# A quarter of two state-space scans' input products moved from VectorE to GpSimd, with two smaller moves to ScalarE and TensorE

## The chip, the cores and the metric

The program runs on one core of a Trainium2 chip. The metric is the device time of one execution in microseconds (us), median of several runs. A core has five engines with queues of their own that meet at semaphores: TensorE (PE in the profile, PEld its weight loads), VectorE (DVE), ScalarE (ACT), GpSimd (POOL) and SyncE (SP, which issues DMAs). SBUF is the working memory of 128 partitions; PSUM holds eight banks of 512 float32 columns, into which TensorE writes.

## The reference

The model is a decoder of four layers with three blocks each, twelve in all, on x of 16 sequences x 128 tokens x 256 features. The change touches two of the twelve, both state-space blocks: the first block of layer 1 (L1_attn, "mamba" in the code) and the first block of layer 3 (L3_attn, "sequence_ssm"). Of the first the reference computes

```python
xc = causal_depthwise_conv(x_inner, conv_w) + conv_b      # 4 taps, 512 channels
x_conv = silu(xc)
ssm = x_conv @ W_xproj;  dt_raw, Bp, Cp = ssm[..., :1], ssm[..., 1:17], ssm[..., 17:]
dt = softplus(dt_raw @ W_dt + b_dt);  A = -exp(A_log)
A_bar = exp(dt * A)                                        # one for each of 16 states
B_bar = (dt * x_conv)[..., None] * Bp[:, :, None, :]
h = A_bar_t * h + B_bar_t                                  # over the tokens
y = sum over states of h * C,  plus  x_conv * D
y = y * silu(z);  out = residual + y @ W_out
```

The second has the same recurrence with 256 channels, a 3-tap convolution across channels made by TensorE, and a normalization behind the gate.

## The kernel before

The twelve blocks run as twelve stages one after another, with a barrier between two. Within a state-space stage the 16 sequences go through in four groups of 4; the tokens of a group stand side by side, 512 columns. Channels lie on partitions, 128 to a block. L1_attn has 4 blocks of channels and takes them two at a time, so its scan runs over 4 groups x 2 halves x 16 states = 128 steps; L3_attn has 2 blocks and runs 4 x 16 = 64 steps. Sixteen steps with the same channels are called a unit here, and four steps in a row (0 to 3, 4 to 7, ...) a quartet.

`class Scan` holds what one step N does, on tiles of 128 x 1024 float32 (two blocks of channels by 512 columns):

- TensorE spreads the row of B for this state over all partitions into one PSUM bank ("brow", L1162) and the row of C into another ("crow"); each of the two has one bank only, and brow N+1 waits until brow N has been read.
- ScalarE makes the decay exp(dt*A) ("decay", two instructions, L1179, two buffers) and copies the row of C to SBUF ("ccol", L1185).
- VectorE multiplies dtx by the row of B into a pair of PSUM banks ("drive", L1195, one buffer) and runs the recurrence ("scan", L1203) with the decay from SBUF and the drive from PSUM; the state goes to one of three SBUF buffers.
- GpSimd multiplies the state by the row of C in place ("weigh", L1210).
- TensorE adds the weighed state to the unit's sum y in PSUM by two matmuls with the identity ("sum", L1168).

Behind the sixteenth sum VectorE runs "finish" (L1415, L1419 in L1_attn; L1711, L1715 in L3_attn): xc*D + y in two instructions, then times the gate. Around the scan stands the work of the next and the last group: the projections and their reads ("inner", "gate", "turn", "project", "delta", "out"; L1281, L1294, L1308), the convolution ("conv", in L1_attn one tensor_scalar L1392 and three scalar_tensor_tensor L1395 on VectorE for each block of channels), "silu" (two ACTIVATEs between two table loads, L1340 to L1342), "relu" (eight ACTIVATEs, L1353, L1354), "soften" (L1360, L1362), the norm's "stats" and "apply" (L241, L261), "rows" and "split" (L1400, L1143 to L1152), "step" and "strength" on GpSimd.

The order in which each engine issues all this is fixed by tables of due times (MAMBA_BY_STEP, MAMBA_BY_GROUP, SSM_BY_STEP and so on): all steps are sorted by due time, in units of a step, and every engine issues its own in that order. An engine never overtakes its own queue: when one instruction waits, all behind it wait.

## Time and profile before

| | us |
|---|---|
| median of 3 runs | 3912.26 |
| lowest and highest of them | 3909.07, 3914.52 |
| the profiled execution's own time | 3913.75 |
| its span | 3912.4 |
| stretch of L1_attn (1210 to 1845), VectorE busy in it | 635, of it 553.0 |
| stretch of L3_attn (3110 to 3500), VectorE busy in it | 390, of it 301.7 |

The span is the time from the first to the last instruction; the execution's own time is 1.35 us more. The page gives busy times of the whole program; since stages follow each other behind barriers, a stage's length counts in full, and what bounds it is read from its own stretch.

### The profile page before, as it was taken

Reading aid. Unit: us, or ns where it says so; the run is one execution under the profiler, and the core shown is the slowest. Engines: PE = TensorE matmul, PEld = TensorE weight load, DVE = VectorE, ACT = ScalarE, POOL = GpSimd, SP = SyncE. Lnnn points to the kernel's source line nnn. Section 1 sums busy time; section 2 is a strip of 40 time slices with the busy share of each in tenths; the row PEclk is TensorE's granted clock in tenths of the full one; section 3 lists DMA queues with packets and bytes.
Section 4 is the critical chain, followed back from the end, with each engine's and each line's share of the span. In section 5 each row is a group of like instructions: output and inputs, shape, how many; then the busy total and the mean of one; then the engine's idle time right before and its main releaser. Section 6 shows DMA issues by size and latency. Waiting matters only on the chain. (4 is left out here: it accounts for less than half of the span.)

```text
span 3912.4 us, 52926 instructions
## 1 busy us (share of the span) xinstructions
PE 3102.8 (79%) x17627; PEld 1971.6 (50%) x17627; DVE 2347.5 (60%) x6436; ACT 1637.3 (42%) x3689; POOL 1450.2 (37%) x1121
## 2 busy tenths in 40 slices
PE   6989986877942777775899999468789678868898
PEld 4666665656631232322666766245567423325655
DVE  6988984374333999997244343544542268874553
ACT  4776763211212556553344444315602145435521
POOL 3777774103443566564122222300010145640020
PEclk7999998888976999999999999789969888889999
DMA  3000000302442000000000000120121200000000
GB/s 100 6 10 7 10 10 22 127 22 78 128 117 86 0 1 0 1 0 16 2 8 1 1 1 1 20 85 26 39 92 29 60 23 1 1 30 2 2 1 22
DMA packets 70999, 116.10 MB, mean 30 GB/s; under 512 B 28688, under 2 KB 58408, under 8 KB 67984
## 3 DMA queue, kind: packets, MB, share of 16 engines
q1 hardware_dynamic: 61184, 86.63, 6.6%
q0 software_dynamic: 9552, 26.10, 2.7%
q8 instruction: 149, 2.44, 0.3%
q14 instruction: 114, 0.93, 0.1%
HBM read 88.71 MB, written 23.99 MB: 29 GB/s over the span
## 5 line engine op out<-in xcount | busy, mean ns | idle before, releaser
L1210 POOL TENSOR_TENSOR L_attn_state<-L_attn_state,L_attn_ccol 128x1024 f32<-128x1024 f32 x192 | 451.8, 2354 | 317.4 <-DVE L_attn_state L1203 242.6
L1168 PE MATMUL bank<-L_attn_state,ident 128*128 128x512 f32 x768 | 404.8, 652 | 90.5 <-POOL L_attn_state L1210 86.5
L1203 DVE TENSOR_TENSOR_SCAN L_attn_state<-L_attn_decay,bank 128x1024 f32<-128x1024 f32 x192 | 438.6, 2284 | 20.1 <-ACT L_attn_decay L1179 1.0
L1179 ACT ACTIVATE L_attn_decay<-L_attn_dt,L_attn_A 128x512 f32<-128x512 f32 x384 | 256.3, 717 | 128.4 <-DVE L_attn_state L1203 120.1
L1168 PEld LDWEIGHTS bank<-L_attn_state,ident 128*128 128x128 f32 x768 | 144.1, 201 | 272.2 <-POOL L_attn_state L1210 149.0
L1107 POOL TENSOR_TENSOR L_xattn_prob<-L_xattn_prob,L_xattn_inv 128x1024 f32<-128x1024 f32 x64 | 121.1, 1893 | 410.1 <-DVE L_xattn_inv L1090 410.1
L1195 DVE TENSOR_TENSOR bank<-L_attn_dtx,bank 128x1024 f32<-128x1024 f32 x192 | 235.6, 1227 | 44.9 <-PE bank L1162 20.3
L1185 ACT COPY L_attn_ccol<-bank 128x512 f32<-128x512 f32 x192 | 112.3, 585 | 226.0 <-PE bank L1162 179.2
L2758 POOL TENSOR_TENSOR L_attn_t<-L_attn_t,L_attn_base 128x1024 f32<-128x1024 f32 x96 | 182.5, 1901 | 37.5 <-DVE L_attn_base L2707 36.8
L1162 PE MATMUL bank<-L_attn_parts,L_attn_select 96*128 96x512 bf16 x384 | 128.2, 406 | 84.6 <-DVE bank L1195 80.8
L758 ACT ACTIVATE L_xattn_prob<-bank,L_xattn_top 128x128 f32<-128x128 f32 x512 | 142.0, 377 | 57.3 <-DVE L_xattn_top L807 56.9
L1032 ACT ACTIVATE L_xattn_prob<-L_xattn_masked,L_xattn_low 128x256 f32<-128x256 f32 x256 | 128.1, 507 | 83.5 <-DVE L_xattn_low L1085 83.5
L1085 DVE CUSTOM_DVE_ANT_0 L_xattn_masked<-bank,L_xattn_hidden 128x256 f32<-128x256 f32 x256 | 96.6, 419 | 105.1 <-PE bank L945 105.1
L2762 POOL TENSOR_TENSOR L_attn_t<-L_attn_t 128x512 f32<-128x512 f32 x96 | 122.0, 1271 | 97.8 <-ACT L_attn_t L2566 97.0
L2711 DVE MATCH_REPLACE8 L_attn_t<-L_attn_top,L_attn_t 128x64 f32<-128x64 f32 x768 | 150.2, 207 | 0.0
L1162 PEld LDWEIGHTS bank<-L_attn_parts,L_attn_select 96*128 96x128 bf16 x384 | 32.5, 102 | 227.0 <-DVE bank L1195 165.2
L3411 POOL DMA_INDIRECT L_ffn_xh<-L_ffn_rows,L_ffn_tokens x96 | 90.9, 947 | 142.0 <-PE bank L3216 80.1
L922 PE MATMUL bank<-L_xattn_kvT,L_xattn_wk 128*128 128x256 f32 x512 | 126.1, 389 | 10.8 <-ACT L_xattn_qT L1020 5.1
L931 PE MATMUL bank<-L_xattn_wv,L_xattn_kvT 128*128 128x512 f32 x256 | 126.9, 618 | 2.2 <-DVE L_xattn_kT L987 0.8
L807 DVE TENSOR_REDUCE L_xattn_top<-bank 128x4 f32<-128x512 f32 x128 | 82.5, 684 | 50.5 <-PE bank L666 50.5
L252 POOL TENSOR_TENSOR L_ffn_norm_rs<-L_ffn_norm_mv,eps 128x4 f32<-128x4 f32 x16 | 5.1, 318 | 289.4 <-DVE L_ffn_norm_mv L245 289.4
L922 PEld LDWEIGHTS bank<-L_xattn_kvT,L_xattn_wk 128*128 128x128 f32 x512 | 92.1, 190 | 32.0 <-ACT L_xattn_qT L1020 11.6
(597 smaller groups left out, 7463.0 us busy)
## 6 DMA issues: line engine op xcount, KB each, us to landing
L_ffn_ew<-in_L_ffn_experts SPq DMA_DIRECT2D x4, 3072.0 KB, 21.0
L_ffn_made<-L_ffn_yout SPq DMA_DIRECT2D x24, 512.0 KB, 2.9
L_ffn_w<-in_L_ffn_w SPq DMA_DIRECT2D x4, 2048.0 KB, 15.1
L_xattn_ctx<-in_ctx_rows SPq DMA_DIRECT2D x3, 2048.0 KB, 8.5
L_ffn_rows<-L_ffn_xh SPq DMA_DIRECT2D x8, 512.0 KB, 2.9
L_ffn_made<-L_ffn_yout SPq DMA_DIRECT2D x11, 256.0 KB, 2.1
L_attn_rows<-in_x SPq DMA_DIRECT2D x16, 128.0 KB, 7.2
turned<-L_attn_rows SPq DMA_DIRECT2D x16, 128.0 KB, 2.3
```

What stands on the lines that cost most here:

```text
L758: t = act.activation(prob[u % 2][j][:, i, :], score[j].bank(u)[:, i * P:(i + 1) * P], ACT.Exp, bias=top[:, j, i:i + 1])
L922: t = pe.matmul(side.bank(at)[:, i * 2 * P:(i + 1) * 2 * P], w["wk"][:, k, col:col + P], kvT[a % 2][:, k, :], start=k == 0, stop=k == KC - 1)
L931: t = pe.matmul(side.bank(at)[:, :], kvT[a % 2][:, k, half * P:(half + 1) * P], w["wv"][:, k, cols], start=k == 0, stop=k == KC - 1)
L1032: t = act.activation(prob[i % 3][:, h, :], masked[i % 2][:, h, :], ACT.Exp, bias=low[:, i % 2, h:h + 1], scale=-1.0, accum_out=total[:, i ...
L1162: pe.matmul(fills.bank(N)[:, :], self.select[:, first + n, :], parts[:, :], start=True, stop=True).then_inc(*fills.full.up())
L1168: t = pe.matmul(self.y[unit % len(self.y)][m][:, :], self.c.ident[:, :], self.state[N % 3][:, m, :], start=n == 0, stop=n == 15)
L1179: t = act.activation(self.decay[N % 2][:, m, :], dt[:, m, :], ACT.Exp, scale=A[:, m, n:n + 1])
L1195: dve.tensor_tensor(self.drive[:, :, :], dtx[:, :, :], self.brow.bank(N)[:, :].unsqueeze(1).broadcast_to([P, 2, GT]), ALU.mult).then_inc(* ...
L1203: dve.tensor_tensor_scan(flat(self.state[N % 3]), flat(self.decay[N % 2]), flat(self.drive), 0.0, ALU.mult, ALU.add).then_inc(*self.scanne ...
L1210: pool.tensor_tensor(state[:, :, :], state[:, :, :], self.ccol[N % 2][:, :].unsqueeze(1).broadcast_to([P, 2, GT]), ALU.mult).then_inc(*sel ...
L2711: m = dve.match_replace(t[n % RING][:, 1, i, :], top[n % 2][:, i, :], t[n % RING][:, 0, i, :], -1e30)
L2758: pool.tensor_tensor(both, both, base[n % 2][:, :].unsqueeze(1).unsqueeze(3).broadcast_to([P, 2, per, nkeys]), ALU.subtract).then_inc(*shi ...
```

## The change

Of each quartet of steps the fourth (N = 3, 7, 11, ...) gets its drive from another engine. ScalarE copies the row of B from its bank to SBUF ("bcol"), GpSimd multiplies dtx by the copy into one SBUF tile ("offer"), and VectorE's scan of that step reads both inputs from SBUF. The offer waits for the scan of the quartet before, which read the same tile, and for the copy. The state gets a fourth buffer, the decay a third.

In L1_attn the convolution's first tap with its bias becomes an ACTIVATE on ScalarE ("tap"), which writes xc; VectorE keeps the three others. In both stages the term xc*D becomes two matmuls with a diagonal matrix that open the unit's sum; the matrices are made by four (L1_attn) or two (L3_attn) tensor_scalar of 128 x 128 at the stage's start. "finish" is then one instruction, the sum from PSUM times the gate, and the next unit's sum waits for it. All tables of due times have new values.

```diff
 class Scan:
+    SHARE = 4
...
-        self.brow, self.crow = Fills(s, "brow", banks[0:1], "v"), Fills(s, "crow", banks[1:2], "a")
+        self.brow, self.crow = Fills(s, "brow", banks[0:1], "vvva"), Fills(s, "crow", banks[1:2], "a")
...
+    def shared(self, N):
+        return N % self.SHARE == self.SHARE - 1
...
+        for m in range(self.blocks):
+            dve.tensor_scalar(self.skip[:, m, :], self.c.ident[:, :], through(m), None, ALU.mult)
...
+            if n == 0:
+                for m in range(2):
+                    pe.matmul(self.y[unit % len(self.y)][m][:, :], self.skip[:, first_block + m, :], past[:, m, :], start=True, stop=False)
...
-            if N >= 2:
-                act.wait_ge(*self.scanned.at(N - 2))
+            if N >= 3:
+                act.wait_ge(*self.scanned.at(N - 3))
...
+        elif what == "bcol":
+            if N >= self.SHARE:
+                act.wait_ge(*self.offered.at(N // self.SHARE - 1))
+            act.wait_ge(*self.brow.filled(N))
+            act.copy(self.bcol[:, :], self.brow.bank(N)[:, :]).then_inc(*self.brow.done(N))
...
-        if what == "drive":
+        if what == "drive" and not self.shared(N):
...
-                dve.wait_ge(*self.scanned.at(N - 1))
+                dve.wait_ge(*self.scanned.at(N - 2 if self.shared(N - 1) else N - 1))
...
-            if N >= 3:
-                dve.wait_ge(*self.summed.at(N - 3))
+            if N >= 4:
+                dve.wait_ge(*self.summed.at(N - 4))
             dve.wait_ge(*self.decayed.at(N))
-            dve.wait_ge(*self.brow.emptied(N))
-            dve.tensor_tensor_scan(flat(self.state[N % 3]), flat(self.decay[N % 2]), flat(self.drive), 0.0, ALU.mult, ALU.add).then_inc(*self.scanned.up())
+            if self.shared(N):
+                dve.wait_ge(*self.offered.at(N // self.SHARE))
+                drive = self.offer
+            else:
+                dve.wait_ge(*self.brow.emptied(N))
+                drive = self.drive
+            dve.tensor_tensor_scan(flat(self.state[N % 4]), flat(self.decay[N % 3]), flat(drive), 0.0, ALU.mult, ALU.add).then_inc(*self.scanned.up())
...
+        if what == "offer":
+            if N % 16 == self.SHARE - 1:
+                pool.wait_ge(*ready)
+            if N >= self.SHARE:
+                pool.wait_ge(*self.scanned.at(N - self.SHARE))
+            pool.wait_ge(*self.brow.emptied(N))
+            pool.tensor_tensor(self.offer[:, :, :], dtx[:, :, :], self.bcol[:, :].unsqueeze(1).broadcast_to([P, 2, GT]), ALU.mult).then_inc(*self.offered.up())
+        elif what == "weigh":
...
-MAMBA_BY_STEP = {"brow": -1.68, "decay": -1.63, "crow": -0.36, "drive": -0.31, "ccol": -0.23, "scan": 0.17, "sum": 0.97, "weigh": 4.34}
+MAMBA_BY_STEP = {"brow": -1.77, "decay": -0.98, "crow": -0.8, "drive": -0.57, "scan": 0.32, "ccol": 0.73, "sum": 1.18, "weigh": 4.13}
+MAMBA_BY_SHARE = {"bcol": 2.15, "offer": 6.12}
...
+        elif what == "tap":
...
+            act.activation(xc[g % 2][:, m, :], side.bank(at)[:, :], ACT.Identity, bias=bias, scale=last).then_inc(*tapped.up())
...
         elif what == "finish":
             g, half = divmod(n, 2)
+            dve.wait_ge(*shaped.at(g))
             dve.wait_ge(*scan.summed.at(16 * n + 15))
-            for i in range(2):
-                m = 2 * half + i
-                t = dve.scalar_tensor_tensor(xc[g % 2][:, m, :], xc[g % 2][:, m, :], w["cols"][:, m, taps + 2:taps + 3], scan.y[0][i][:, :], ALU.mult, ALU.add)
-            t.then_inc(*finished.up())
-            dve.wait_ge(*shaped.at(g))
-            dve.wait_ge(*finished.at(n))
-            dve.tensor_tensor(halves(xc[g % 2], half), halves(xc[g % 2], half), halves(z[g % 2], half), ALU.mult).then_inc(*gated.up())
+            dve.tensor_tensor(halves(xc[g % 2], half), c.twins[0][:, :, :], halves(z[g % 2], half), ALU.mult).then_inc(*gated.up())
```

Three places show how the order moves. In all of them the scan is printed as SCALAR_TENSOR_TENSOR, the number behind L_attn_state tells the buffer (before 18127 to 18129, now 18128 to 18131, whose last is always a fourth step's), and bank stands for PSUM.

VectorE, steps 120 to 123 of L1_attn, before:

```order
L1195 TENSOR_TENSOR bank<-L_attn_dtx_18117,bank 128x1024
L1203 SCALAR_TENSOR_TENSOR L_attn_state_18127<-L_attn_decay_18125,bank 128x1024
L1195 TENSOR_TENSOR bank<-L_attn_dtx_18117,bank 128x1024
L1203 SCALAR_TENSOR_TENSOR L_attn_state_18128<-L_attn_decay_18126,bank 128x1024
L1195 TENSOR_TENSOR bank<-L_attn_dtx_18117,bank 128x1024
L1203 SCALAR_TENSOR_TENSOR L_attn_state_18129<-L_attn_decay_18125,bank 128x1024
```

and now:

```order
L1213 TENSOR_TENSOR bank<-L_attn_dtx_18117,bank 128x1024
L1226 SCALAR_TENSOR_TENSOR L_attn_state_18129<-L_attn_decay_18126,bank 128x1024
L1213 TENSOR_TENSOR bank<-L_attn_dtx_18117,bank 128x1024
L1226 SCALAR_TENSOR_TENSOR L_attn_state_18130<-L_attn_decay_18127,bank 128x1024
L1226 SCALAR_TENSOR_TENSOR L_attn_state_18131<-L_attn_decay_18125,L_attn_offer 128x1024
L1213 TENSOR_TENSOR bank<-L_attn_dtx_18117,bank 128x1024
```

The fourth step's drive is gone, its scan follows the third's directly, and the next quartet's drive stands behind it.

GpSimd at the same steps, before:

```order
L1210 TENSOR_TENSOR L_attn_state_18127<-L_attn_state_18127,L_attn_ccol_18130 128x1024
L1210 TENSOR_TENSOR L_attn_state_18128<-L_attn_state_18128,L_attn_ccol_18131 128x1024
L1210 TENSOR_TENSOR L_attn_state_18129<-L_attn_state_18129,L_attn_ccol_18130 128x1024
L1210 TENSOR_TENSOR L_attn_state_18127<-L_attn_state_18127,L_attn_ccol_18131 128x1024
```

and now:

```order
L1240 TENSOR_TENSOR L_attn_state_18128<-L_attn_state_18128,L_attn_ccol_18132 128x1024
L1240 TENSOR_TENSOR L_attn_state_18129<-L_attn_state_18129,L_attn_ccol_18133 128x1024
L1236 TENSOR_TENSOR L_attn_offer<-L_attn_dtx_18117,L_attn_bcol 128x1024
L1240 TENSOR_TENSOR L_attn_state_18130<-L_attn_state_18130,L_attn_ccol_18132 128x1024
L1240 TENSOR_TENSOR L_attn_state_18131<-L_attn_state_18131,L_attn_ccol_18133 128x1024
```

The offer stands between the second and the third step's weigh in every quartet of both stages.

TensorE at the end of L1_attn's third unit (steps 45 to 49); L_attn_w_ssm marks "project", which waits for silu, and L_attn_skip the new matmuls. Before:

```order
L1168 MATMUL bank<-L_attn_state_18129,ident 128x512 x2
L1162 MATMUL bank<-L_attn_parts_18119,L_attn_select_18124 128x512
L1294 MATMUL bank<-L_attn_xc_18112,L_attn_w_ssm 32x512 x2
L1162 MATMUL bank<-L_attn_parts_18119,L_attn_select_18124 128x512
L1168 MATMUL bank<-L_attn_state_18127,ident 128x512 x2
```

and now:

```order
L1326 MATMUL bank<-L_attn_xc_18112,L_attn_w_ssm 32x512 x2
L1181 MATMUL bank<-L_attn_state_18131,ident 128x512 x2
L1172 MATMUL bank<-L_attn_parts_18119,L_attn_select_18124 128x512 x2
L1178 MATMUL bank<-L_attn_xc_18113,L_attn_skip 128x512 x2
L1181 MATMUL bank<-L_attn_state_18128,ident 128x512 x2
```

Before, the project stood behind the unit's last sum (state 18129 is step 47's); now it stands ahead of it (18131 is step 47's).

## Rows read from the trace of the kernel before

**Rows 1.** The page's head: span, and busy time of each engine in the whole program.

```profile
span 3912.4 us, 52926 instructions
PE 3102.8 (79%) x17627; PEld 1971.6 (50%) x17627; DVE 2347.5 (60%) x6436; ACT 1637.3 (42%) x3689; POOL 1450.2 (37%) x1121
```

**Rows 2.** Busy time by stretch: L1_attn, then L3_attn; clock, DMA share, GB/s last.

```profile
1210.00:1845.00 635.00, 457.17 (x1120) 176.78 (x1120) 553.02 (x436) 325.59 (x490) 352.65 (x192) 0.93 0.02 8
3110.00:3500.00 390.00, 288.55 (x700) 118.10 (x700) 301.74 (x372) 175.11 (x286) 208.01 (x143) 0.86 0.04 10
```

**Rows 3.** Groups in L1_attn: busy us, mean ns | idle before, and its releasers.

```profile
L1210 POOL TENSOR_TENSOR L_attn_state<-L_attn_state,L_attn_ccol 128x1024 f32<-128x1024 f32 x128 | 301.3, 2355 | 210.0 <-DVE L_attn_state L1203 144.2 <-ACT L_attn_ccol L1185 65.6
L1203 DVE TENSOR_TENSOR_SCAN L_attn_state<-L_attn_decay,bank 128x1024 f32<-128x1024 f32 x128 | 292.5, 2285 | 15.4 <-ACT L_attn_decay L1179 1.0
...
L1195 DVE TENSOR_TENSOR bank<-L_attn_dtx,bank 128x1024 f32<-128x1024 f32 x128 | 157.1, 1227 | 16.6 <-POOL L_attn_dt L1467 10.7 <-PE bank L1162 1.7
...
L1392 DVE TENSOR_SCALAR L_attn_xc<-bank,L_attn_cols 128x512 f32<-128x512 f32 x16 | 12.8, 798 | 7.6 <-PE bank L1281 7.6
L1354 ACT ACTIVATE L_attn_soft<-bank,L_attn_cols,L_attn_w_dt 128x512 f32<-128x512 f32 x16 | 12.6, 789 | 0.0
...
L1415 DVE SCALAR_TENSOR_TENSOR L_attn_xc<-L_attn_xc,L_attn_cols,bank 128x512 f32<-128x512 f32 x16 | 11.2, 743 | 6.0 <-PE bank L1168 6.0
...
L1360 ACT ACTIVATE L_attn_soft<-L_attn_soft 128x1024 f32<-128x1024 f32 x8 | 8.5, 1057 | 0.0
...
L1400 DVE COPY L_attn_bc<-bank 32x512 f32<-32x512 f32 x4 | 2.7, 680 | 17.2 <-PE bank L1294 17.2
```

**Rows 4.** The same view of L3_attn: first the drives, then the finish's first part.

```profile
L1195 DVE TENSOR_TENSOR bank<-L_attn_dtx,bank 128x1024 f32<-128x1024 f32 x64 | 78.5, 1226 | 28.3 <-PE bank L1162 18.6 <-POOL L_attn_dt L1791 7.9
...
L1711 DVE SCALAR_TENSOR_TENSOR L_attn_h<-L_attn_h,L_attn_cols,bank 128x512 f32<-128x512 f32 x8 | 5.6, 744 | 5.4 <-PE bank L1168 5.4
```

**Rows 5.** Timeline of one plain step of L1_attn: start us, duration us, engine, instruction.

```profile
1809.15 1.23 DVE L1195 TENSOR_TENSOR bank<-L_attn_dtx,bank 128x1024 f32<-128x1024 f32 x1
1809.26 2.35 POOL L1210 TENSOR_TENSOR L_attn_state<-L_attn_state,L_attn_ccol 128x1024 f32<-128x1024 f32 x1 [1.33 <-DVE L_attn_state L1203]
...
1810.43 0.60 PE L1162 MATMUL bank<-L_attn_parts,L_attn_select 96*128 96x512 bf16 x2 [0.46 <-DVE bank L1195]
1810.51 2.29 DVE L1203 TENSOR_TENSOR_SCAN L_attn_state<-L_attn_decay,bank 128x1024 f32<-128x1024 f32 x1
1811.13 0.58 ACT L1185 COPY L_attn_ccol<-bank 128x512 f32<-128x512 f32 x1 [0.65 <-PE bank L1162]
...
1811.66 1.98 PE L1168 MATMUL bank<-L_attn_state,ident 128*128 128x512 f32 x4 [0.62 <-POOL L_attn_state L1210]
...
1812.83 1.23 DVE L1195 TENSOR_TENSOR bank<-L_attn_dtx,bank 128x1024 f32<-128x1024 f32 x1
```

**Rows 6.** All executions of L1985, with two SBUF inputs: ns min/median/max.

```profile
L1985 DVE SCALAR_TENSOR_TENSOR L_ffn_h<-L_ffn_h,L_ffn_h x32: 691/693/1886, 3726.7 to 3888.6; 128x512 f32<-128x512 f32 x32
```

**Rows 7.** Timeline of the last stage: VectorE's L1985 beside GpSimd's L2006, L2008, L2010.

```profile
3739.84 1.89 POOL L2006 TENSOR_TENSOR L_ffn_twice<-L_ffn_val,L_ffn_bo 128x1024 f32<-128x1024 f32 x1 [15.29 <-DVE L_ffn_hot L1954]
...
3740.40 1.88 DVE L1985 SCALAR_TENSOR_TENSOR L_ffn_h<-L_ffn_h,L_ffn_h 128x512 f32<-128x512 f32 x1
...
3741.81 2.22 POOL L2008 TENSOR_TENSOR L_ffn_twice<-L_ffn_twice 128x1024 f32<-128x1024 f32 x1
...
3742.91 1.67 DVE L1985 SCALAR_TENSOR_TENSOR L_ffn_h<-L_ffn_h,L_ffn_h 128x512 f32<-128x512 f32 x1
...
3744.11 2.69 POOL L2010 TENSOR_TENSOR X<-X,L_ffn_twice 128x1024 f32<-128x1024 f32 x1
```

**Rows 8.** Timeline of L1_ffn: VectorE starts 0.08 us behind GpSimd.

```profile
2495.38 2.12 POOL L2157 TENSOR_TENSOR L_ffn_yb<-L_ffn_yb,L_ffn_bias 128x1024 bf16<-128x1024 bf16 x1 [7.43 <-ACT L_ffn_yb L2111]
2495.46 2.59 DVE L2138 TENSOR_SCALAR L_ffn_over<-L_ffn_big 128x1024 f32<-128x1024 fp8e4 x1
```

**Rows 9.** Timeline of L1_attn: apply, beside two weighs in a row.

```profile
1290.80 4.69 POOL L1210 TENSOR_TENSOR L_attn_state<-L_attn_state,L_attn_ccol 128x1024 f32<-128x1024 f32 x2
...
1292.15 3.50 DVE L261 TENSOR_SCALAR L_attn_xn<-X,L_attn_norm_mv,L_attn_norm_rs 128x256 f32<-128x256 f32 x2
```

**Rows 10.** ScalarE's timeline at a silu.

```profile
1495.62 1.28 ACT L1340 ACT_TABLE_LOAD   x1
1496.91 1.91 ACT L1340 ACTIVATE L_attn_xc<-L_attn_xc 128x2048 f32<-128x2048 f32 x1
```

More of the change, by code:

```diff
@@ L1479, in ssm_weights @@
             ("a_log", name + "_a_log", [P, KC, NSTATE], F32), ("select", "select", [6 * NSTATE, 2 * NSTATE], F32)]
[L1482 to L1488 removed]
+SSM_BY_STEP = {"decay": -2.15, "weigh": -1.52, "drive": -1.23, "brow": -0.98, "crow": -0.55, "scan": -0.46, "ccol": -0.23, "sum": 1.78}
+SSM_BY_SHARE = {"offer": -0.22, "bcol": 1.77}
+SSM_BY_GROUP = {"stats": -25.24, "square": -19.99, "root": -18.09, "whole": -16.63, "wholes": -16.43, "apply": -15.55, "turned": (-14.21, -12.6),
+                "turn": (-13.85, -13.01), "inner": (-10.8, -9.91), "pad": (-10.61, -10.39), "shift": -10.46, "conv": (-9.86, -9.1),
+                "rooted": (-9.38, -9.13), "moved": -8.34, "normal": (-8.32, -8.1), "back0": -8.05, "convs": (-7.81, -7.41), "ranks": -7.11,
+                "rows": -6.81, "silu": -6.3, "rank": -6.1, "project": -5.77, "delta": (-5.72, -4.33), "step": -5.54, "strength": -5.44,
+                "split": -4.51, "relu": (-4.22, -3.91), "soften": -3.61, "finish": 16.03, "moments": (16.85, 17.44), "back": (17.83, 18.39),
+                "lastroot": 18.2, "last": 19.26, "out": (19.42, 20.18), "add": (19.74, 21.11)}
 def sequence_ssm(c, s, w, name, taps=3, rank=16):
@@ L1573, in tensor @@
             unit = n // 16
[L1574 removed]
+            scan.tensor(what, n, parts[unit % 2], scan.parted.at(unit), gated.at(unit - 1) if unit else None, h[unit % 2], 0)
         elif what == "back":
```

119 lines of the change are left out of this document (59 added, 60 removed).

## The prediction

> **What bounds the kernel now.** I read the page's head first [rows 1]: VectorE is the busiest engine but TensorE, at 60% of the span. Stages follow behind barriers, so what counts is each of the two stretches [rows 2]. In L1_attn VectorE is busy 553.0 of 635 us, in L3_attn 301.7 of 390, GpSimd 352.7 and 208.0: VectorE bounds both, GpSimd has room. The groups say with what [rows 3]: 128 scans of 2285 ns and 128 drives of 1227 ns. Then one plain step in order of time [rows 5]: a drive starts at 1809.15, the next at 1812.83, so a step lasts 3.68 us: drive 1.23, scan 2.29, two handovers of together 0.16. The weigh (2.35) waits for its scan [rows 3, 5] and is hidden. The execution took 3913.75, which is 1.35 over its span and 1.5 over the median; I sum against it and take 1.5 off at the end.
>
> **A plain quartet, step by step.** Let D be the end of the third step's drive. Before: third scan D+0.13 to 2.42, fourth drive 2.45 to 3.68, fourth scan 3.81 to 6.10.
>
> After, first the offer's own chain. The fourth brow is free to start at D+0.05 and takes a matmul, about 0.35 (two take 0.60, rows 5). The copy to SBUF takes as long as ccol's, 0.58, and ends near D+1.12. GpSimd is not free then: the second step's weigh starts 0.11 behind its scan's end, which is D−1.25 or so, and ends at D+1.22. So the offer runs 1.25 to 3.60. No row shows a GpSimd product with a broadcast SBUF operand except the weigh, which has this very form and size, so I price the offer at 2.35. The scan could start at D+3.65 and end at 5.94, **0.16 earlier** than now. The drive taken away (1.23) is thus nearly all given back as a wait for GpSimd.
>
> Second, the fourth scan reads decay and offer, both in SBUF; the plain scan has one input in PSUM. The trace has no such scan, but it has another VectorE operation with two SBUF inputs, L1985: 691 ns at least, 1886 at most [rows 6]. In the long cases GpSimd was at work [rows 7]: L2006 ends at 3741.73, and L1985, started at 3740.40, ends at 3742.28, 0.55 later, about its own 0.69. The second ends at 3744.58, again 0.55 behind L2008's end (3744.03). It waited for the whole GpSimd instruction. The other way holds too: L2010, started during such an L1985, took 2.69 where its like take 1.9 to 2.2. And where GpSimd starts first by only 0.08, VectorE's instruction is the one that is held [rows 8].
>
> The place: at the offer's end the third weigh stands directly behind it in GpSimd's queue, and all it waits for has been there since D+2.5. Two weighs in a row are recorded as 4.69 for both [rows 9], with no gap; a VectorE instruction released by GpSimd starts about 0.05 later. So the weigh is first, 3.60 to 5.95, the scan is held and ends 2.29−0.14 behind it, at 8.10 instead of 6.10: **+2.0 us for a plain quartet**.
>
> The Trainium skill, "SBUF — State Buffer", § Who interferes with whom, says the same for a DVE instruction with two SBUF inputs against a GpSimd instruction that reads SBUF, and that whoever issues first has the pair for its whole instruction. Its page "Advanced Engine Details and Errata", § VectorE Performance Modes, names only "2p Vector instructions" as blocked; by that, an fp32 scan would run free and the sum would be that of the second case below; rows 6 and 7 speak against it.
>
> **The quartets of L1_attn, 32.** Where other VectorE work stands in the quartet, GpSimd gets its weighs and the offer done meanwhile.
> - 21 have none: 21 × 2.0 = +42.
> - 8 have conv, stats, or rows and split: the offer is ready beforehand, the scan follows the third one and starts before the weigh, so each gains the drive with its handover, 1.33: −10.6. If they collide as well, 8 × 2.0 more.
> - 3 have apply, which by itself blocks and is blocked by GpSimd (3.50 for two, the weighs 4.69 beside it, rows 9): +0.8 each, +2.5.
>
> **The other parts in L1_attn.**
> - Tap: 16 tensor_scalar of 798 ns leave VectorE [rows 3]. The first four, in the prologue, wait for TensorE anyway (7.6 idle before the sixteen): 0. The other 12 × 0.80 = −9.6. ScalarE is busy 326 of 635 [rows 2] and takes 12 × 0.8, the price of relu's ACTIVATE of that shape from a bank (789).
> - Finish: two instructions of 743 go and one handover, two-input 128x1024 from PSUM stays like a drive: 8 × 1.35 = −10.8. For it TensorE makes 16 more matmuls of 512 columns, 0.5 each by the sum's 1.98 for four [rows 5]. TensorE is busy 457 of 635; they open the sum when the bank is free, hidden.
> - Rows waits 17.2 for its project now [rows 3], part of it outside the prologue; the new table puts it five steps later: −3.4. Set-up matrices: +1.
> - New stalls. Project now stands ahead of the unit's last sum on TensorE, and project waits for silu: decay, table load 1.28, 1.91 [rows 10], project 1.9, then sum 1.98, and finish behind it: 3 × 1.15 = +3.5. Relu's eight ACTIVATEs and soften's 1057 stand ahead of the next decay: with one decay of lead gained by the third buffer I get 3 × 2.5 = +7.5. Out ahead of sum and brow: +3. Brow late behind the new inner order: +2.5. Together +16.5; from 0 (the third buffer covers all) to 25.
>
> L1_attn: 42 − 10.6 + 2.5 − 9.6 − 10.8 − 3.4 + 1 + 16.5 = **+27.6**.
>
> **L3_attn, 16 quartets.** Its drives already wait 28.3 in all, 18.6 of it for brow [rows 4]. Three are plain (+6). Four have some VectorE work, half covered (+2). Three have rows or ranks beside them (−3). In three, at the turn of a unit, strength and the norm's powers stand on GpSimd ahead of the offer, and brow stands behind whole; the scan waits for two GpSimd instructions more: +6, +6, +4. Three with moments: +1. Finish, 4 × (2 × 0.744 plus a handover, less what waits for the last sum, 5.4 in all [rows 4]) is −2. Together **+20**.
>
> **Sum.** 27.6 + 20 = +47.6; 3913.75 + 47.6 − 1.5 = 3959.9, so **3960**, 1.2% slower. Own range: if the stalls don't come (−16.5) and L3's unit turns cost nothing (−16) 3928; if the eight covered quartets and three of L3 collide too (11 × 2.35 = +26), and a few us of stalls come on top, 3990.
>
> **Rivals.**
> - *The shared scan isn't held*: it goes in first, or two SBUF inputs don't block a scan. Then plain quartets gain 0.16 (21 × 0.16 = −3.4), apply costs nothing, L1_attn is −3.4 − 10.6 − 22.8 + 16.5 = −20.3. L3_attn: 20 less 6.5 (plain), 3 (half covered), 6 (turns) and 1: +3.5. Together −16.8: **3896**. This ends on the other side; it decides on 0.09 us, the handover to VectorE against GpSimd's own next instruction. For it: in rows 7 a VectorE instruction that was waiting got in before L2008. Against: L2008 was itself waiting for L2006's result; the weigh waits for nothing. 0.12.
> - *As that, and the third decay buffer covers the new stalls*: −33, **3879**. 0.03. VectorE would then really be lighter by what it lost.
> - *The blocking reaches the covered quartets as well*: GpSimd runs 160 weighs and offers at 2.35 in some 650 us, more than half the time, so a shared scan that comes at any moment is likelier than not to find one running. Against: in those eight the scan's place is right behind the third scan, ahead of the weigh that this one releases. +26: **3986**, within my range. 0.15.
> - *The clock*: TensorE is granted 0.93 and 0.86 in the two stretches [rows 2]. Longer waits in every quartet could bring it down; sums and brows, now hidden under a 3.68 us step, would then be 4 us each. In plain quartets its idle time grows from some 1.1 to 1.6 us a step. I take it as a small part of the stalls above, with no case of its own.
>
> **How the numbers follow.** Held scans 0.85 (0.70 as summed, 0.15 with the covered ones), the other two 0.12 and 0.03. The likeliest gives 3960. The range must reach the 0.12 case: **3890 to 3990**; below it lies the 0.03, above it a tail of the stalls, beside a share of the first rival's spread. A measurement can tell some 0.2%, 8 us. Faster: 0.03 + 0.10; same: 0.02 of the second case and 0.03 where the held scans cost half of what I say; slower: 0.82.
>
> **What would show it.** The 48 shared scans as a group by their form: mean near 4.4 us where they collide, 2.3 where not, and idle before them of 1.2 behind the offer. The timeline of a plain quartet: offer, weigh at once, scan's end 2.15 behind the weigh's. Offers of 2.35. Idle before finish (behind sum), before the scans of the steps behind relu (behind decay), and the wait for offer at L3's unit turns. The tap near 0.8 and the finish near 1.25 with no wait. It is wrong if the shared scans have a mean below 3 us, or if they start ahead of the third weigh.

## The result, and the profile after

| | before | after |
|---|---|---|
| median, us (4 runs each) | 3913.16 | 3959.56 |
| lowest and highest | 3909.07, 3914.52 | 3958.05, 3963.91 |
| ratio, 95% interval | | 1.0124, 1.0108 to 1.014 |
| profiled span | 3912.4 | 3956.8 |
| first to last scan of L1_attn | 552.3 | 579.8 |
| first to last scan of L3_attn | 311.5 | 337.3 |

The change makes the kernel slower by 46 us, 1.2%; the forecast was 3960. The two stretches from the start of the first scan to the end of the last give +27.5 and +25.8 us, together 53.3; outside them the profiled run is some 9 us shorter than before (3.2 ahead of the first scan, 3.0 between the stretches, 2.9 behind them). The stretches are the measure below: what lies between them holds of the change only L1_attn's last finish and L3_attn's set-up, and still takes anything from 1340.7 to 1349.7 us in the kernels below, so a median alone would hide small terms.

The page's head after, to be held against [rows 1]:

```profile
span 3956.8 us, 53092 instructions
PE 3134.2 (79%) x17675; PEld 1985.4 (50%) x17675; DVE 2330.3 (59%) x6354; ACT 1664.0 (42%) x3753; POOL 1597.6 (40%) x1169
```

VectorE is busy 17 us less and the program is 44 us longer. GpSimd has 147 us more; only 113 of them are the 48 offers (2.355 each), of the rest 24 are longer weighs (in L1_attn 313.8 instead of 301.3, in L3_attn 161.7 instead of 150.5) and 8 longer products for dtx. What VectorE does in L1_attn between its first and last scan is the view that answers to [rows 3] (groups, here with VectorE alone: busy us, mean ns | idle before, its releasers):

```profile
L1226 DVE TENSOR_TENSOR_SCAN L_attn_state<-L_attn_decay,bank 128x1024 f32<-128x1024 f32 x96 | 219.2, 2283 | 11.8 <-ACT L_attn_decay L1192 2.8 <-DVE bank L1213 0.5
L1226 DVE TENSOR_TENSOR_SCAN L_attn_state<-L_attn_decay,L_attn_offer 128x1024 f32<-128x1024 f32 x32 | 118.6, 3706 | 35.8 <-POOL L_attn_offer L1236 35.7
L1213 DVE TENSOR_TENSOR bank<-L_attn_dtx,bank 128x1024 f32<-128x1024 f32 x95 | 116.0, 1221 | 17.6 <-PE bank L1172 15.7
L261 DVE TENSOR_SCALAR L_attn_xn<-X,L_attn_norm_mv,L_attn_norm_rs 128x256 f32<-128x256 f32 x12 | 9.8, 872 | 0.0
...
L1452 DVE TENSOR_TENSOR L_attn_xc<-bank,L_attn_z 128x1024 f32<-128x1024 f32 x7 | 8.6, 1222 | 2.6 <-PE bank L1181 2.6
...
L1438 DVE COPY L_attn_bc<-bank 32x512 f32<-32x512 f32 x3 | 2.0, 653 | 0.0
```

The same view of before has for the drives and for the finish's first part:

```profile
L1195 DVE TENSOR_TENSOR bank<-L_attn_dtx,bank 128x1024 f32<-128x1024 f32 x127 | 155.9, 1227 | 5.9 <-PE bank L1162 1.7
...
L1415 DVE SCALAR_TENSOR_TENSOR L_attn_xc<-L_attn_xc,L_attn_cols,bank 128x512 f32<-128x512 f32 x14 | 9.8, 742 | 1.4 <-PE bank L1168 1.4
```

Read together, L1_attn's 27.5 us are: drives 155.9 to 116.0, −39.9; waits for the offer +35.7, with other waits before scans down by 3.6 (15.4 to 11.8); scans 292.5 to 337.8, **+45.3**, though their number is the same 128; waits before drives 5.9 to 17.6, +11.7; taps −9.5; finish −9.8 busy (the first parts are gone), +0.5 waiting; rows' wait −4.1; apply +2.6. (These add up to 29; records of instructions in a row overlap by some hundredths each.) The scans that got longer are the 32 that read the offer, mean 3706 against 2283 ns of the others.

One quartet, L1_attn's last, in order of time (start us, duration us, engine, instruction):

```profile
1842.63 1.23 DVE L1213 TENSOR_TENSOR bank<-L_attn_dtx,bank 128x1024 f32<-128x1024 f32 x1
1842.74 2.34 POOL L1240 TENSOR_TENSOR L_attn_state<-L_attn_state,L_attn_ccol 128x1024 f32<-128x1024 f32 x1 [1.33 <-DVE L_attn_state L1226]
...
1843.99 2.29 DVE L1226 TENSOR_TENSOR_SCAN L_attn_state<-L_attn_decay,bank 128x1024 f32<-128x1024 f32 x1
1844.39 0.59 ACT L1198 COPY L_attn_bcol<-bank 128x512 f32<-128x512 f32 x1 [2.37 <-PE bank L1172]
...
1845.12 2.34 POOL L1236 TENSOR_TENSOR L_attn_offer<-L_attn_dtx,L_attn_bcol 128x1024 f32<-128x1024 f32 x1
...
1847.42 2.34 POOL L1240 TENSOR_TENSOR L_attn_state<-L_attn_state,L_attn_ccol 128x1024 f32<-128x1024 f32 x1
...
1847.60 4.31 DVE L1226 TENSOR_TENSOR_SCAN L_attn_state<-L_attn_decay,L_attn_offer 128x1024 f32<-128x1024 f32 x1 [1.32 <-POOL L_attn_offer L1236]
```

D is 1843.86. The offer starts at D+1.26 and the scan at D+3.74. The third weigh started 0.18 before the scan and ends at 1849.76; the scan ends at 1851.91, 2.15 later, D+8.05. A plain quartet, one in which VectorE has nothing but drives and scans, lasts 16.56 instead of 14.72 to 14.79.

In ten quartets of L1_attn the scan comes first. In seven of them VectorE had other work ahead, so that the offer was ready. In the other three (1, 9 and 17, counted from 0 as everywhere below) VectorE waited for the offer, but the third weigh still waited for its copy of the row of C and started 0.60 behind the offer's end, when the scan, 0.13 behind it, had begun. The quartet with the four convs of L1_attn's first unit:

```profile
1318.90 2.35 POOL L1236 TENSOR_TENSOR L_attn_offer<-L_attn_dtx,L_attn_bcol 128x1024 f32<-128x1024 f32 x1
...
1319.75 2.28 DVE L1226 TENSOR_TENSOR_SCAN L_attn_state<-L_attn_decay,bank 128x1024 f32<-128x1024 f32 x1
...
1321.94 2.27 DVE L1226 TENSOR_TENSOR_SCAN L_attn_state<-L_attn_decay,L_attn_offer 128x1024 f32<-128x1024 f32 x1
1322.17 6.51 POOL L1240 TENSOR_TENSOR L_attn_state<-L_attn_state,L_attn_ccol 128x1024 f32<-128x1024 f32 x2 [0.92 <-DVE L_attn_state L1226]
```

Here the scan has its 2.27 and the two weighs take 6.51 instead of 4.69 [rows 9]: now they are held. Of the 32 shared scans of L1_attn 22 lasted 4.31 to 4.47 and 10 lasted 2.26 to 2.29; of L3_attn's 16 it was 8 and 8 (the short ones 2.25 to 2.29).

### The profile page after: what moved, and what is told of

Read it like the earlier page. It is cut to its first block and busy times, and to the rows that moved or that the text cites. A ratio compares the mean times of both kernels' runs of the same rounds, so it can differ in the third digit from the quotient of the medians.

```text
span 3956.8 us, 53092 instructions
## 1 busy us (share of the span) xinstructions
PE 3134.2 (79%) x17675; PEld 1985.4 (50%) x17675; DVE 2330.3 (59%) x6354; ACT 1664.0 (42%) x3753; POOL 1597.6 (40%) x1169
## 5 line engine op out<-in xcount | busy, mean ns | idle before, releaser
L1240 POOL TENSOR_TENSOR L_attn_state<-L_attn_state,L_attn_ccol 128x1024 f32<-128x1024 f32 x192 | 475.4, 2480 | 199.7 <-DVE L_attn_state L1226 164.4
L1181 PE MATMUL bank<-L_attn_state,ident 128*128 128x512 f32 x768 | 430.7, 689 | 127.4 <-POOL L_attn_state L1240 127.2
L1226 DVE TENSOR_TENSOR_SCAN L_attn_state<-L_attn_decay,bank 128x1024 f32<-128x1024 f32 x144 | 328.7, 2282 | 15.2 <-ACT L_attn_decay L1192 2.8
L1181 PEld LDWEIGHTS bank<-L_attn_state,ident 128*128 128x128 f32 x768 | 154.5, 213 | 321.1 <-POOL L_attn_state L1240 185.7
L1213 DVE TENSOR_TENSOR bank<-L_attn_dtx,bank 128x1024 f32<-128x1024 f32 x144 | 175.8, 1221 | 47.0 <-PE bank L1172 26.8
L1226 DVE TENSOR_TENSOR_SCAN L_attn_state<-L_attn_decay,L_attn_offer 128x1024 f32<-128x1024 f32 x48 | 171.3, 3569 | 53.8 <-POOL L_attn_offer L1236 46.3
L1172 PE MATMUL bank<-L_attn_parts,L_attn_select 96*128 96x512 bf16 x384 | 136.5, 409 | 78.4 <-DVE bank L1213 45.3
L922 PE MATMUL bank<-L_xattn_kvT,L_xattn_wk 128*128 128x256 f32 x512 | 126.1, 389 | 10.8 <-ACT L_xattn_qT L1020 5.1
L1236 POOL TENSOR_TENSOR L_attn_offer<-L_attn_dtx,L_attn_bcol 128x1024 f32<-128x1024 f32 x48 | 113.0, 2354 | 21.0 <-ACT L_attn_bcol L1198 20.0
```

What stands on the lines that cost most here:

```text
L922: t = pe.matmul(side.bank(at)[:, i * 2 * P:(i + 1) * 2 * P], w["wk"][:, k, col:col + P], kvT[a % 2][:, k, :], start=k == 0, stop=k == KC - 1)
L1172: pe.matmul(fills.bank(N)[:, :], self.select[:, first + n, :], parts[:, :], start=True, stop=True).then_inc(*fills.full.up())
L1181: t = pe.matmul(self.y[unit % len(self.y)][m][:, :], self.c.ident[:, :], self.state[N % 4][:, m, :], start=False, stop=n == 15)
L1213: dve.tensor_tensor(self.drive[:, :, :], dtx[:, :, :], self.brow.bank(N)[:, :].unsqueeze(1).broadcast_to([P, 2, GT]), ALU.mult).then_inc(* ...
L1226: dve.tensor_tensor_scan(flat(self.state[N % 4]), flat(self.decay[N % 3]), flat(drive), 0.0, ALU.mult, ALU.add).then_inc(*self.scanned.up())
L1240: pool.tensor_tensor(state[:, :, :], state[:, :, :], self.ccol[N % 2][:, :].unsqueeze(1).broadcast_to([P, 2, GT]), ALU.mult).then_inc(*sel ...
```

## The experiments

Eleven kernels, each timed against the kernel before on the same chip. Stretches are those of the first to the last scan, in us, each from one profile. L3_attn's code is the same in e4 and e9 and took 305.4 and 309.1, so differences under 4 us there show nothing; L1_attn's is the same in e3 and e9 and took 540.2 and 540.0.

| | ratio, 95% interval | L1_attn | L3_attn |
|---|---|---|---|
| before | | 552.3 | 311.5 |
| after | 1.0124 (1.0108 to 1.014) | 579.8 | 337.3 |
| e1, shared scan reads a bank | 0.9926 (0.9909 to 0.9942) | 543.3 | 309.4 |
| e2, third weigh behind the scan | 1.0184 (1.0167 to 1.0201) | 598.0 | 346.7 |
| e3, no sharing | 0.9918 (0.9902 to 0.9935) | 540.2 | 309.0 |
| e4, no sharing, old due times | 0.9945 (0.9929 to 0.9962) | 549.7 | 305.4 |
| e5, e2 with later sums | 1.0216 (1.0197 to 1.0236) | 591.5 | 360.6 |
| e6, shared row early | 1.0282 (1.0261 to 1.0303) | 580.3 | 398.9 |
| e7, before with tap | 0.9973 (0.9963 to 0.9983) | 544.6 | 312.8 |
| e8, before with skip | 0.9988 (0.9978 to 0.9997) | 558.0 | 305.4 |
| e9, no sharing, a table each | 0.9940 (0.9925 to 0.9955) | 540.0 | 309.1 |
| e10, small fill ahead of the weigh | 1.0157 (1.0138 to 1.0177) | 590.1 | 339.9 |
| e11, e10 with rows ahead of sums | 1.0245 (1.0228 to 1.0262) | 598.6 | 366.7 |

**e1: is it the two SBUF inputs?**

```diff
             if self.shared(N):
                 dve.wait_ge(*self.offered.at(N // self.SHARE))
-                drive = self.offer
+                drive = self.drive
```

(The next drive waits for this scan too.)

> The changed kernel, but each fourth scan takes its drive from the PSUM pair that the third step's drive has filled, and not from GpSimd's tile in SBUF; it still waits for the offer, which is made as before, and only its result isn't used (so those steps' states are not the reference's). Theory (the scan is held because both of its inputs are in SBUF): all 48 shared scans last 2.29; 29 of them lasted 4.3 to 4.5, so 29 x 2.05 = 59 us go, 3900 +- 6. Rival (the scan is long for another reason, such as the wait for the offer or GpSimd being busy at all): the shared scans stay near 4.3 in plain quartets and the time near 3960.

The ratio times 3913 is 3884, 76 us under the changed kernel against 59 expected (30 scans had been held, not 29). The scans in L1_attn's stretch, all of one form now:

```profile
L1226 DVE TENSOR_TENSOR_SCAN L_attn_state<-L_attn_decay,bank 128x1024 f32<-128x1024 f32 x128 | 292.1, 2284 | 45.3 <-POOL L_attn_offer L1236 33.4 <-ACT L_attn_decay L1192 2.8 <-DVE bank L1213 0.5
```

The mean is 2284 for all 128, though GpSimd makes every offer and weigh and the wait for the offer is still there (33.4). The weighs of L1_attn are back at 300.7 us as well. Only the place of one input and the next drive's wait changed, so the 4.3 us are due to the two SBUF inputs. The stretches fall by 36.5 and 27.9, together 64. In L1_attn the scans give 45.7 and longer waits before drives and finish take part of it back; in L3_attn the scans give 16.9, and another 6.2 come from a second instruction with two SBUF inputs, split's TENSOR_TENSOR (L1155): 2.72 each in the changed kernel, 0.68 here and before. e1 also says what the sharing is worth with the hold gone: 852.7 for both stretches, against 849.1 without sharing (e3). The drive that VectorE gives away comes back as the wait.

**e2: does the order at the offer's end decide?**

```diff
             pool.wait_ge(*self.crow.emptied(N))
-            pool.wait_ge(*self.scanned.at(N))
+            pool.wait_ge(*self.scanned.at(N + 1 if self.shared(N + 1) else N))
```

> The changed kernel, with one wait more: the weigh of each third step waits for the fourth step's scan, so that GpSimd starts nothing between the offer's end and that scan. Theory (who starts first holds the other, and the scan loses by the handover): the scan runs 2.29 right behind the offer, plain quartets last 14.56 instead of 16.56, 29 x 2.0 = 58 us less; two weighs and two sums come later, which may cost a few us at finish and at the unit turns: 3903, 3895 to 3925. Rival (the shared scan is slow beside GpSimd whatever the order, or the two late weighs hold up the next quartet's offer): 3940 to 3965.

The time is a miss: slower than the changed kernel, not 57 us faster, and above the rival's 3965 too. Of the mechanism the first half came: all 48 shared scans last 2.25 to 2.29, and quartets 11 and 19 of L1_attn take 14.61. Near the stretch's end the trace shows what took its place:

```profile
1848.72 2.29 DVE L1226 TENSOR_TENSOR_SCAN L_attn_state<-L_attn_decay,L_attn_offer 128x1024 f32<-128x1024 f32 x1 [1.34 <-POOL L_attn_offer L1236]
...
1851.16 4.65 POOL L1240 TENSOR_TENSOR L_attn_state<-L_attn_state,L_attn_ccol 128x1024 f32<-128x1024 f32 x2 [2.57 <-DVE L_attn_state L1226]
...
1853.56 3.78 PE L1181 MATMUL bank<-L_attn_state,ident 128*128 128x512 f32 x4 [4.89 <-POOL L_attn_state L1240]
1857.13 1.06 PE L1172 MATMUL bank<-L_attn_parts,L_attn_select 96*128 96x512 bf16 x2
...
1858.30 1.23 DVE L1213 TENSOR_TENSOR bank<-L_attn_dtx,bank 128x1024 f32<-128x1024 f32 x1 [3.74 <-PE bank L1172]
```

TensorE stands 4.89 us at the third step's sum, with the next rows of B and C queued behind it; then the sum takes 3.78 instead of 1.98, since the granted clock of that stretch is 0.50 (the lower of its two levels, 1.2 GHz) where the steps around have 1.00 (2.4 GHz). The next drive waits 3.74 for its row.

```profile
1853.50:1857.20 3.70, 3.64 (x5) 1.38 (x6) 1.06 (x1) 0.00 (x0) 2.31 (x2) 0.50 0.00 0
1860.96:1862.90 1.94, 1.94 (x6) 0.75 (x5) 1.91 (x2) 1.82 (x3) 0.81 (x1) 1.00 0.00 0
```

(Length; busy time of PE, PEld, DVE, ACT, POOL; granted clock; DMA share, GB/s.) Before it fell TensorE had been idle for 4.89 us, since the two rows that ended at 1848.67.

**e10: the same question with a tenth of a microsecond.**

```diff
             pool.tensor_tensor(self.offer[:, :, :], ...).then_inc(*self.offered.up())
+            pool.memset(self.spacer[:, :], 0.0)
```

> The changed kernel with one small instruction more: GpSimd fills a tile of 256 columns that nobody reads, between the offer and the third step's weigh. Nothing else waits for it, so it only moves the weigh's start by a few tenths of a us behind the offer's end, past the 0.13 at which the scan starts. Theory (whoever starts first has both inputs' way for its whole instruction): all 48 shared scans last 2.29, and it is the weigh that is held, its record 2.1 longer; the late weigh then holds the third step's sum and the rows queued behind it, as in the run with the explicit wait, so the time is about that run's, 3991, 3970 to 4000. Rival (a scan with two SBUF inputs is slowed by whatever GpSimd does, in either order): shared scans stay near 4.3, time near 3960 + 48 x 0.3 = 3974.

```profile
1846.13 0.32 POOL L1238 MEMSET L_attn_spacer<- 128x256 f32 x1
...
1846.33 2.29 DVE L1227 TENSOR_TENSOR_SCAN L_attn_state<-L_attn_decay,L_attn_offer 128x1024 f32<-128x1024 f32 x1 [1.33 <-POOL L_attn_offer L1237]
1846.40 6.66 POOL L1242 TENSOR_TENSOR L_attn_state<-L_attn_state,L_attn_ccol 128x1024 f32<-128x1024 f32 x2
```

The scan starts 0.07 before the weigh and has its 2.29; the two weighs take 6.66. In the changed kernel the weigh was 0.18 ahead and the scan took 4.31. So whichever starts first keeps the way for its whole length, and it is shown from both sides: here all 48 shared scans start ahead of the next weigh and last 2.25 to 2.29; in the changed kernel each of the 30 held ones starts 0.03 to 0.19 behind a weigh. The fill, which only writes, held nobody: the scan started in the middle of it and was not longer. The total, 3975 on the chip where before took 3913.5, is within what was expected, but the rival's total (3974) is too, so it is the scans' length that decides between them. VectorE's wait before drives in L1_attn is why nothing is won:

```profile
L1214 DVE TENSOR_TENSOR bank<-L_attn_dtx,bank 128x1024 f32<-128x1024 f32 x95 | 116.1, 1222 | 63.8 <-PE bank L1173 62.5
L1227 DVE TENSOR_TENSOR_SCAN L_attn_state<-L_attn_decay,L_attn_offer 128x1024 f32<-128x1024 f32 x32 | 73.1, 2286 | 34.4 <-POOL L_attn_offer L1237 34.3
```

46 us gained on the scans, 46 lost before the drives (17.6 to 63.8), 7 more at the finish.

**e5 and e11: can TensorE's order give it back?** e5 makes the sums due later in e2, e11 the rows of B earlier in e10.

```diff
-MAMBA_BY_STEP = {"brow": -1.77, ..., "sum": 1.18, "weigh": 4.13}
+MAMBA_BY_STEP = {"brow": -1.77, ..., "sum": 1.3, "weigh": 4.13}      # e5; second stage 1.78 to 2.05
+MAMBA_BY_STEP = {"brow": -1.85, ..., "sum": 1.18, "weigh": 4.13}     # e11; second stage -0.98 to -1.25
```

> The run with the weigh behind the shared scan was slower, though its shared scans lasted 2.29 and some quartets 14.61: in the others TensorE stood at the third step's sum, which waits for the late weigh, and the next row of B was queued behind it, so the next drive waited 3.7. Here the same kernel with the sums due 0.12 (second stage 0.27) of a step later, which puts the next rows ahead of that sum. Theory (the order of TensorE took back what the order of GpSimd gave): nearly all plain quartets 14.6, scans' stretches together some 865 instead of 945, 3908, 3895 to 3925. Rival (two weighs in a row behind the scan are themselves too late, by the buffers or GpSimd's load): over 3940.

> The run with the small fill between offer and weigh, and in TensorE's order one thing more: each row of B stands one place earlier, ahead of the sum of three steps before instead of behind it (due 0.08 earlier in the first stage, 0.27 in the second); sums and all else keep their places. Theory (what the free scan won was lost at the rows queued behind the late sum): VectorE's 63.8 us of idle before drives in the first stage fall to about 20, plain quartets are 14.5 throughout, the first stage's stretch is near 550 and the time 3925, 3905 to 3945. Even then it isn't under the run without sharing (3890), since the scan still waits some 1.3 for each offer. Rival (the late weigh is itself what binds): no less than 3960.

Both totals are misses, by 87 and 84 us. In e5 seven plain quartets of L1_attn are what was expected, 14.51 to 14.55, but the first quartet of six of the seven later units takes 22.6 to 24.9 and of the last 19.4 (17.8 to 19.7 in the changed kernel). In e11 the wait before drives did fall from 63.8 to 18.0, and came up elsewhere:

```profile
L1214 DVE TENSOR_TENSOR bank<-L_attn_dtx,bank 128x1024 f32<-128x1024 f32 x95 | 116.2, 1223 | 18.0 <-PE bank L1173 16.0
L1227 DVE TENSOR_TENSOR_SCAN L_attn_state<-L_attn_decay,L_attn_offer 128x1024 f32<-128x1024 f32 x32 | 73.2, 2288 | 56.0 <-POOL L_attn_offer L1237 49.9 <-PE bank L1182 6.0
...
L1454 DVE TENSOR_TENSOR L_attn_xc<-bank,L_attn_z 128x1024 f32<-128x1024 f32 x7 | 8.6, 1225 | 29.8 <-PE bank L1182 29.8
```

The finish waits 29.8 instead of 10.0. In TensorE's order a row now stands ahead of the unit's last two sums, and in four of the seven units it waits 3.65 for a drive, with the sums queued behind it; in the three others the project stands there too. The scans wait 56.0, 49.9 of it for offers. In these two attempts one due time for all steps did not serve both a plain quartet and a unit's end. My reading of e10 as "only the rows behind the late sum" was too narrow: with the rows out of the way the wait came back at the finish and before the offers, so the late weigh costs there as well.

**e6: sharing with the row first.** ScalarE's copy is made from the second row of a quartet, the offer stands between two pairs of weighs, the third step's weigh waits for the shared scan as in e2, and a table of four due times each for rows and sums follows.

```diff
+        return N - N % self.SHARE + (0, 2, 3, 1)[N % self.SHARE]        # place of a step's row in the bank
...
-MAMBA_BY_SHARE = {"bcol": 2.15, "offer": 6.12}
+MAMBA_BY_SHARE = {"bcol": -0.1, "offer": 3.6, "brow": (-2.1, -0.2, 0.1, 1.35), "crow": (-0.85, 0.7, 1.4, 2.5), "sum": (2.14, 2.8, 4.22, 4.8)}
```

> An attempt to make sharing pay: the shared step's row of B is the second of its quartet in the bank, not the fourth, so ScalarE's copy is early; GpSimd's order is weigh, weigh (third and fourth step of the quartet before), offer, weigh, weigh; the third step's weigh waits for the shared scan; rows and sums of TensorE are put where these come free. A plain quartet then costs GpSimd 5 x 2.35 and the scan's 2.15 to itself, 13.95, against 14.72 of before and 16.56 of the changed kernel. If it works 0.75 x some 45 quartets under the kernel without sharing (3890): 3857, 3840 to 3890. If the tight order makes new waits at the quartets with other work, 3890 to 3930; the plain quartets' length tells the mechanism by itself.

A few plain quartets came near the plan: 13.90 in L3_attn, and 13.91, 14.21 and 14.52 among those of L1_attn's last two units, at best 0.8 under before. The order isn't what it should be either: 15 of the 48 shared scans still last 2.5 to 3.9. The total is a miss by 166 us: the third quartets of L3_attn's first three units, those with rows and ranks, take 43.6 to 45.3, against 29 to 32 before. So sharing won up to 0.8 us in single plain quartets, and this order lost far more elsewhere; which part of it lost that was not taken apart.

**e3, e4, e9: the change without sharing.**

```diff
     def shared(self, N):
-        return N % self.SHARE == self.SHARE - 1
+        return False
```

(No bcol, no offer, every row emptied by VectorE. e4 has the due times of before in both stages, e9 in the second stage.)

> The changed kernel without the sharing: all drives on VectorE again, no bcol, no offer; tap on ScalarE, skip term on TensorE, three decay and four state buffers and all new due times stay. By the terms of the sum, tap -9.6 and some -3 in the prologue, finish -10.8 and -2, rows -3.4, set-up +1, stalls of the new order +16.5: 3913 - 11 = 3902. If the stalls don't exist without the sharing: 3886. Rival (tap and skip bring nothing on the path): 3913 to 3930.

> As the run without the sharing, but with the due times of the kernel before (tap just ahead of its conv). Tap -9.6 and -3 in the prologue, finish -10.8 and -2, set-up +1, no new stalls and no gain at rows: 3913 - 24 = 3889. The difference to the run with the new due times is what these cost by themselves: 13 by my terms. If the new due times cost nothing by themselves, both give the same.

> No sharing, tap on ScalarE and skip term on TensorE, the new due times in the first stage and those of before in the second. The scans' stretches were 540.2 (new due times) and 305.4 (old ones) in the two runs that had each: together 845.6 against 863.7 of before and 849.1 of the run with new due times in both. So 18 under before by the stretches, some 4 under the run without sharing; ratio 0.994 or below. If other stages' noise is larger, 0.991 to 0.998.

All three are faster than before, by 0.8, 0.55 and 0.6%; e3 and e9 can't be told apart and are the best kernels of this study. The sharing alone is thus the changed kernel less e3: 39.6 + 28.3 = 68 us in the stretches (the ratios, 1.0124 and 0.9918, say 81 of the total), and the rest of the change is worth −15 us in the stretches (the ratio of e3 says −32 of the total). e3 came out at 3890 where 3902 was expected, e4 at 3899 where it was 3889. The new due times gain 9.5 us in L1_attn without the sharing where I had them cost 13. For e9 the 3.6 us that e4's L3_attn had been shorter did not come back: the same code took 305.4 in one run and 309.1 in another, so that step of the expectation rested on noise; its total, 0.9940, is as expected.

**e7 and e8: tap alone, skip alone**, each with the due times of before.

> The kernel before with the first tap on ScalarE alone. By my terms 12 x 0.80 = 9.6 less in the scan's stretch and some 3 less ahead of it: 3913 - 12 = 3901. If conv waits for ScalarE instead (a tap queued behind a decay), under 4 us less.

> The kernel before with the skip term on TensorE alone (with the four state and three decay buffers of the changed kernel). By my terms 8 x 1.35 = 10.8 in the first stage and 2 in the second less, set-up +1: 3913 - 12 = 3901. In the run with both edits and the old due times every second quartet behind a finish was 1.7 longer than before, so part is given back there: 3 to 4 us of it.

The tap is worth 7.7 us in the stretch (expected 9.6), and the ratio gives 10.6 (3899 measured, 3901 expected). The skip term is worth 5 us by its ratio, 0.9988 (3905 measured, 3901 expected, 3 to 4 more if part is given back). L3_attn is 6.1 shorter, not much more than the same code varies, but L1_attn becomes 5.7 *longer*. Finish falls from 2.7 to 1.2 as expected, and in VectorE's groups this appears beside it:

```profile
L1213 DVE TENSOR_TENSOR bank<-L_attn_dtx,bank 128x1024 f32<-128x1024 f32 x127 | 155.8, 1227 | 12.8 <-PE bank L1172 8.9
...
L1448 DVE TENSOR_TENSOR L_attn_xc<-bank,L_attn_z 128x1024 f32<-128x1024 f32 x7 | 8.5, 1220 | 1.5 <-PE bank L1181 1.5
...
L1434 DVE COPY L_attn_bc<-bank 32x512 f32<-32x512 f32 x3 | 2.0, 679 | 13.8 <-PE bank L1326 13.8
```

Rows waits 13.8 for its project instead of 4.1, drives wait 12.8 instead of 5.9. The turn behind L1_attn's third unit shows how:

```profile
1500.91 1.88 PE L1178 MATMUL bank<-L_attn_xc,L_attn_skip 128*128 128x512 f32 x4
...
1502.63 1.88 PE L1181 MATMUL bank<-L_attn_state,ident 128*128 128x512 f32 x4
...
1504.44 1.90 PE L1326 MATMUL bank<-L_attn_xc,L_attn_w_ssm 128*32 128x512 f32 x4
...
1506.38 0.68 DVE L1434 COPY L_attn_bc<-bank 32x512 f32<-32x512 f32 x1 [4.49 <-PE bank L1326]
```

The skip matmuls stand ahead of sum and project on TensorE; before, the project started at 1502.82 and rows at 1504.76, with a wait of 1.26. VectorE reached this place earlier by the shorter finish, and waits until TensorE is through. With the new due times (e3) rows waits nothing, as rows stands five steps later.

## Why the prediction was right

The mechanism forecast as the likeliest is the one that occurred, and that the kernel becomes about 1% slower follows from it. That the number was right to a microsecond is luck, as its own steps show:

- **The sum.** e3 parts each stretch. In L1_attn the sharing is worth +39.6 (42 − 10.6 + 2.5 = 33.9 said) and the rest −12.1 (−6.3 said): two errors of 6 us that cancel. In L3_attn the sharing is worth +28.3 (22 said) and the rest −2.5 (−2 said). Together the stretches grew by 53.3 where 47.6 was said, and what lies outside them, for which next to nothing was said, came out some 9 shorter in the profiled run, which no run explains.
- **The quartet's clock held**: offer from D+1.26 (1.25), scan's start D+3.74 (3.65), end D+8.05 (8.10). The handover from GpSimd's product to the scan is 0.13, not 0.05 (behind GpSimd's small instructions the trace of before has 0.03 to 0.10), so the scan loses the race by more than I took. A plain quartet grew by 1.84 at most, not 2.0: the held scan ends 0.05 earlier than I said, and the next drive, which no longer waits for the scan just ahead of it, starts 0.08 before that scan's recorded end instead of 0.03 behind it.
- **The hold held.** e1 removes it by the place of one input, e2 and e10 by the order of the starts, with both inputs still in SBUF. L1985's 0.55 behind GpSimd's end [rows 7] was the right row to read: the held scan ends 2.15 behind it, 0.14 less than its own 2.29, as there.
- **The count held, its members did not.** 22 scans of L1_attn were held. Of the 21 quartets that I took as plain 18 were, the other three being those in which the weigh waited for its row of C; of the 8 that I took as covered the two with stats were held (4.41 and 4.32), and six kept their 2.27 to 2.29, with the weigh held instead; of the three with apply two were held.
- **The stalls of +16.5 were of about the right size (14.0) and of the wrong kind.** Waits for decays rose by 1.8 (7.5 said) and the finish waited 0.5 more (3.5 said); what came was +11.7 before the drives. That the skip matmuls are part of it is likely, not shown: with the old due times the skip term makes it 6.9 [e8], with the new ones and no sharing it is 6.8 [e3]. In e1, where no hold covers it, the finish does wait 9.1, 7.0 of it in the three units where the project stands ahead of the last sum: twice what I said for that. In the changed kernel, with its longer quartets, most of it was hidden.
- **Finish and rows.** Finish −9.8 busy for the seven within the stretch (−10.8 said for eight) and rows −4.1 (−3.4 said); but in e8, with rows at its old place, finish's gain is lost again at rows. That moving rows alone brings it back is argued; e3 moves all due times at once. I had called the skip matmuls hidden; with the old order they were not. I had also counted 16 of 0.5 each, but a matmul of the code is two records in the trace (rows 5 has four for the sum's two): the trace has 32, together 17.5 us, twice what I took. That step was wrong in its reason.
- **Prologue**: 3.2 us less in the profiled run (I said 0 and +1). But the kernels with the tap on ScalarE have their first scan anywhere from 1266.1 to 1276.6, and the two without it at 1272.5 and 1275.3, so it is not shown.
- **L3_attn +25.8, said +20, by errors that cancel.** The four quartets that I took as half covered (1, 5, 9, 13; said +2) were held, all four, and are longer by 2.6, 5.3, 6.9 and 4.4, together +19.2. The three at the units' ends (3, 7, 11), said +16, are +5.3, and two of their three shared scans weren't held: I had added a wait for brow there, but the waits before drives within the stretch fell from 20.3 to 11.9. The two errors are of the order of the term itself. I had no term for split's TENSOR_TENSOR, which the weighs hold too (8.2 instead of 2.0 for three), and the finish, −2 said (by its own numbers −1.1), gave −3.7. The scans, the drives and split's instruction in the stretch after:

```profile
L1226 DVE TENSOR_TENSOR_SCAN L_attn_state<-L_attn_decay,bank 128x1024 f32<-128x1024 f32 x48 | 109.5, 2281 | 3.4
L1213 DVE TENSOR_TENSOR bank<-L_attn_dtx,bank 128x1024 f32<-128x1024 f32 x47 | 57.3, 1220 | 11.9 <-PE bank L1172 11.1
...
L1226 DVE TENSOR_TENSOR_SCAN L_attn_state<-L_attn_decay,L_attn_offer 128x1024 f32<-128x1024 f32 x16 | 52.8, 3297 | 18.0 <-POOL L_attn_offer L1236 10.7 <-PE bank L1181 7.4
L1155 DVE TENSOR_TENSOR L_attn_rest<-L_attn_bc,L_attn_parts 32x512 f32<-32x512 f32 x3 | 8.2, 2723 | 0.1
```

- **The rival on the other side**, 3896, is what e1 measures: 0.9926 × 3913 = 3884, and −11 us in the stretches where the rival had −16.8. It did not occur because the weigh started 0.18 us ahead.

In L1_attn another VectorE instruction, with one SBUF tile as input, gets longer: apply's 128x256 rises from a mean of 655 to 872, in e10 to 1052. I take it as held by weighs that come closer on each other; no run parts this out. What is open: whether a shared kernel with due times searched anew for its own order could be under e3. The bound from e6's plain quartets is 0.8 each, 38 us for all 48; my three attempts at it, e5, e6 and e11, were slower.

## What to carry to other kernels

Work given from a busy engine to an idle one counts only by when its result is there: here the idle engine's product was ready 3.60 us behind the third drive's end, where VectorE's own had been ready at 3.68, and 1.23 us of work became 1.3 us of waiting. Before moving an operand from PSUM to SBUF, look at what GpSimd runs at that moment: a VectorE instruction with two SBUF inputs and a GpSimd product from SBUF exclude each other whole, and a tenth of a microsecond decides which waits. And when a held instruction is freed, look at the engine that the loser feeds, since its queue may carry the next step's work behind it.
